# Moving the store of the normalised attention output (x1_scr) from GpSimd's DMA queue to ScalarE's

## The reference

```python
c_kv = h @ W_dkv + b_dkv            # 1024 -> 128
c_q  = h @ W_dq + b_dq
k = c_kv @ W_uk + b_uk              # 16 heads of 48, + 16 rotary from h @ W_kr
v = c_kv @ W_uv + b_uv              # 16 heads of 64
q = c_q @ W_uq + b_uq               # + 16 rotary from c_q @ W_qr
attn = softmax(q k^T / 8) v ; attn = attn @ W_o + b_o
x = layernorm(x + attn)
y = x @ int4_quantised(kernel) + bias + (x @ a) @ b
x = layernorm(x + y)
```

## Time and profile before

| | us |
|---|---|
| median of 2 runs | 3198.26 (3198.25 to 3198.28) |
| the profiled execution | 3201.12 |
| its span on the slowest core (core 3) | 3199.5 |
| spans of the other cores | 3168.2 to 3192.4 |

### The profile page before, as it was taken

The page is one execution under the profiler, slowest core; times in us unless marked ns, Lnnn a source line. Parts: engine busy times, 40 slices in busy tenths (PEclk is TensorE's granted clock), DMA queues, the critical chain, the costliest instruction groups (busy, mean ns, idle before and its releaser), DMA issues.

```text
span 3199.5 us, 40217 instructions; the slowest of 8 cores (3168.2 to 3199.5 us)
## 1 busy us (share of the span) xinstructions
PE 2508.0 (78%) x10584; PEld 787.7 (25%) x10584; DVE 1168.8 (37%) x1494; ACT 2193.9 (69%) x2481; POOL 228.0 (7%) x388
## 2 busy tenths in 40 slices
PE   0545759999788978888888888997889788988733
PEld 0222312222232222222222222222222222222211
DVE  3266311212443244324342443244423343334344
ACT  0233339999678976788679867986788677977700
POOL 3000000000000000000000000000000000010000
PEclk9756669999899998899999989998999899999966
DMA  5432230001212111201220121112111212121221
GB/s 94 112 102 97 80 85 19 22 18 35 75 50 71 35 63 56 75 24 49 73 76 29 45 81 48 58 42 71 57 54 50 69 42 65 36 80 44 65 92 40
DMA packets 90051, 190.27 MB, mean 59 GB/s; under 512 B 18643, under 2 KB 50644, under 8 KB 89588
## 3 DMA queue, kind: packets, MB, share of 16 engines
q1 hardware_dynamic: 47812, 86.48, 9.5%
q0 software_dynamic: 28208, 76.05, 8.0%
q10 hardware_dynamic: 13824, 25.17, 2.1%
HBM read 144.65 MB, written 51.64 MB: 61 GB/s over the span
## 4 chain that ended last, share of the span: by engine, by line
PE 54%; DVE 13%; ACT 11%; issue 10%; DMA 10%; SPq 1%; POOL 0%; DVEq 0%; ACTq 0%; POOLq 0%
PE PS L234 51%; ACT Psb L246 8%; DVE tA L251 3%; DVE bcast_sb L277 3%; PE PS L240 2%; ACT bcast_sb L246 2%; DMA h<-h 2%; DMA bcast_sb<-rden 1%; DVE h L251 1%; DMA rotq_scr<-c0s_sb 1%; DMA x_scr<-tA 1%; DMA rden<-bcast_sb 1%; DVE Qsb L257 1%; DMA wbuf<-W_dq 1%; DVE Psb L257 1%
## 5 line engine op out<-in xcount | busy, mean ns | idle before, releaser
L246 ACT ACTIVATE Psb<-PS 128x1024 bf16<-128x1024 f32 x2048 | 1979.8, 1042 | 476.2 <-PE PS L234 462.5
L234 PE MATMUL PS<-Psb,Vsb 128*65 128x512 bf16 x4096 | 1330.5, 408 | 114.2 <-ACT bcast_sb L246 96.5
L234 PE MATMUL PS<-Qsb,Ksb 64*128 64x512 bf16 x4096 | 831.0, 399 | 93.3 <-ACT Psb L246 85.4
L234 PEld LDWEIGHTS PS<-Qsb,Ksb 64*128 64x128 bf16 x4096 | 221.7, 93 | 960.0 <-issue 957.4
L234 PEld LDWEIGHTS PS<-Psb,Vsb 128*65 128x65 bf16 x4096 | 294.2, 112 | 613.8 <-issue 613.8
L277 DVE RECIPROCAL bcast_sb<-bcast_sb 128x512 f32<-128x512 f32 x64 | 214.4, 3350 | 261.4 <-DMA bcast_sb<-rden 261.4
L251 DVE TENSOR_TENSOR tA<-PS,h 128x512 f32<-128x512 f32 x128 | 88.4, 691 | 566.0 <-PE PS L234 526.8
L240 PE MATMUL PS<-ident_sb,h 128*128 128x128 f32 x512 | 106.6, 367 | 187.1 <-DMA h<-h 120.4
L273 DVE CAST oun_sb<-PS 64x512 bf16<-64x512 f32 x128 | 87.4, 682 | 424.6 <-PE PS L234 422.5
L234 PE MATMUL PS<-wbuf,osb 128*128 128x512 bf16 x512 | 169.0, 417 | 73.6 <-DVE tA L251 57.3
L227 POOL DMA_DIRECT2D rden<-bcast_sb x128 | 63.1, 498 | 1595.0 <-ACT bcast_sb L246 1573.1
(11 more groups left out here) (84 smaller groups left out, 1104.9 us busy)
## 6 DMA issues: line engine op xcount, KB each, us to landing
h<-h SPq DMA_DIRECT2D x64, 512.0 KB, 4.3
wbuf<-wo_p POOLq DMA_DIRECT2D x32, 512.0 KB, 5.9
bcast_sb<-rden POOLq DMA_DIRECT2D x128, 128.0 KB, 2.8
x_scr<-tA POOLq DMA_DIRECT2D x32, 512.0 KB, 3.1
wbuf<-wf_p POOLq DMA_DIRECT2D x32, 512.0 KB, 5.6
h<-x_scr SPq DMA_DIRECT2D x32, 512.0 KB, 3.8
out<-tA ACTq DMA_DIRECT2D x32, 512.0 KB, 2.7
o_dram<-oun_sb ACTq DMA_DIRECT2D x64, 128.0 KB, 1.7
```

Of the source, the lines that this page charges most:

```text
L234: e.matmul(o, l, r, start=s1, stop=s2, tile_position=t, skip_group_check=k)),
L246: e.activation(o, i, f, scale=sc, bias=b)),
```

## The change

The issue of the store of `x1_scr` moves from GpSimd's queue to ScalarE's. Its waits, its semaphore and its data stay. It is executed 32 times, 4 in each block.

```diff
@@ -911,7 +911,7 @@
                 for _ in ln_chain_gen(e2["sDV"], par):
                     yield
                 st["h2_free"][par] = st["sq_free"]
-                xw = dma("gpsimd", x1_scr[128 * sub:128 * (sub + 1), :], tA[:, :],
+                xw = dma("scalar", x1_scr[128 * sub:128 * (sub + 1), :], tA[:, :],
                          sem="qX", waits=[("sDV", st["ln_out"])])
                 st["tA_q"] = ("qX", xw["qX"])
                 x1w_s[sub] = xw["qX"]
```

## The result

The change makes the kernel slower by a little: ratio of the times 1.0046, 95% interval 1.0036 to 1.0056, that is 14.7 us (11.5 to 17.9) on 3198 us. The medians are 3220.8 us over 44 runs and 3204.6 us for the kernel before over 42; both contain runs in which one die had the lower clock, and the ratio leaves those out.

What follows compares the result with a forecast made beforehand. No engine saturated: PE and ACT hand tiles over through two PSUM buffers, so the change acts only through waits. 9.5 + 4.5 - 1.9 = +12.1 us on the profiled 3201.1 gives 3213.2; prediction 3210 us, range 3198 to 3221.

Steps and rivals of the forecast that it cites:

- What is special at sub = 2, and how ACT behaves: Third sub-tile, interleaved blocks: reciprocal delays the LayerNorm multiply; ACT waits, next exponential starts 0.60 us after the multiply's end.
- Cost at sub = 2, +9.5: Seven interleaved blocks: new PE stall of 3.64 us, old wait gone, net +1.72 us each, less 2.5: +9.5 us.
- TensorE's clock, +4.5: After the longer PE stalls at sub = 2: more time at the lower clock, 3 sites, +4.5 us, bounds 0 to 14.
- Sub = 0 and 1: nothing: Interleaved blocks' first two sub-tiles: ACT loses at most 0.45 us a store, covered by projection matmuls; zero.
- Sub = 3: nothing: Interleaved blocks' fourth sub-tile: no reciprocal lies between, ACT's loss of at most 0.45 us is covered; zero.
- The last block, -1.9: Last token block, three times: ACT has nothing else to do, write into tA comes sooner, 3.1 us after multiply; -1.9 us.
- POOL and SP: zero: GpSimd loses 32 issues and waits, but nothing behind them starts earlier with effect; SP's x1_scr loads unaffected; zero.
- only the issue counts: Rival, chance 0.17: ACT's wait at sub = 2 is made good in later slack; 3196 us, or up to 3202.
- The activations pass the wait: Rival, chance 0.05: exponentials behind the store run on, waits for tA shrink or vanish; 3176 to 3190 us.
- The clock decides: Rival, chance 0.2: every new stall brings 6 slow us and other sites' 0.45 is not fully covered; 3214 to 3228 us.

Runs made afterwards that it cites:

- wait_only: Kernel before, all stores on GpSimd's queue, plus a bare wait on ScalarE for the multiply at sub = 2 of the seven interleaved blocks; ratio to before 1.0031.
- recip8_act: The change with the pair's reciprocal and multiply recorded one step later on VectorE, all 32 stores on ScalarE; ratio to the kernel before 0.9930.
- not_sub2: The change with the 7 stores at sub = 2 of the interleaved blocks left on GpSimd, 25 moved; ratio to the kernel before 1.0030.

## Why the prediction was right, step by step

The time lies inside the range (12.1 us were forecast, 14.7 measured, which on 3198.3 makes 3213), and the main mechanism is the forecast one. The median after, 3220.8, would be at the very edge of 3198 to 3221; but the forecast started from two runs at 3198.3, and over 42 runs the kernel before has 3204.6. The parts do not all agree, and the total is good in part by luck, since errors offset each other.

- **What is special at sub = 2, and how ACT behaves**: right. The issue came 0.08 us after the multiply (0.07 said), the exponential 0.57 after (0.60), PE's matmul 1.73 after (1.77), and PE's stalls were 3.52 to 4.88 us over all cores (3.6 to 5.4).
- **Cost at sub = 2, +9.5**: right. Over all cores PE's stalls there rose from 2.5 to 3.8 us a place, and the time of the head pair by 10.8 us in all.
- **TensorE's clock, +4.5**: over-sized. From 16 us before the multiply's end to 16 us behind it, the time at the lower level was 6.8 us a place before and 6.2 after; in the 32 us behind it, 10.0 and 10.2. So the longer stall brings no longer slow stretch that can be seen, and the 10.8 us above contain whatever it brings. The step took the new stretches from two windows, and the windows before had 0 to 3.4 us behind stalls of the same 1.92 us; so wide a spread was no basis for a difference. Its upper bound of 14 is also added up wrongly: the long stalls enter it with 1.3 slow us and the others with half of 6.0; with the half in both it is 9 + 2.6 = 11.6.
- **Sub = 0 and 1: nothing**: right for ScalarE's queue, where the exponentials' delay was covered. **Sub = 3: nothing**: the transposes come 0.6 us later than before, which the step did not foresee. What it costs can't be told: of the 15.0 us of attention, about 1 is left for it and everything else.
- **The last block, -1.9**: right. Three times 17.1 became 16.4 us, -2.1, and the first write into tA comes 2.82 us after the multiply (3.1 said).
- **POOL and SP: zero**: wrong, by 6.2 us at the end and by 3.2 in the third interleaved block. The step counted what waits behind GpSimd's stores, and neither what the engine does when it closes nor its late issues, which fall elsewhere when the sequence gets shorter. The trace of the kernel before shows 6.2 us after the last issue (3193.3 to 3199.5), and no step asked what they are made of.

Sum of what was found: 10.8 + 3.2 + 6.2 - 2.1 = 18.1 us, and with the 1 us that is left over 19, as in the profiles without the first phase; the timed runs say 14.7 (11.5 to 17.9). The forecast had about 10 us too little for GpSimd and what is left over, and 3 too much for sub = 2 with its clock; that, and a timed difference below the profiled one, left a total that looks better than its parts.

Of the rivals, "only the issue counts" failed on wait_only and recip8_act. The rule behind it (the Trainium skill, DMA: Bandwidth & Descriptors, "Issuing engines are not separate DMA queues") holds for the transfer, since the issue-to-landing time changed only from 3.1 to 2.7 us; it doesn't speak of what stands behind the wait on the issuing engine, and at sub = 2 that is the cost. "The activations pass the wait" failed on the first timeline after. "The clock decides" has no support in the times at the lower level above.

## What to carry to other kernels

Before a DMA is moved to another engine's queue, look up when its last wait will be met, and what stands behind it in the new queue at that moment: an idle GpSimd can wait for free, and a ScalarE that feeds TensorE can't. When a wait of 4 us appears between two engines, ask what the third engine did in that time; here a 3.35 us reciprocal that nobody needed yet stood ahead of a 0.75 us multiply that two engines needed, and recording it two steps later was worth 2.3%, five times what the queue of the store was worth.

## What the runs showed of the hardware that was not expected

- GpSimd's closing DRAIN takes 3.25 to 9.79 us, by the sequence of DMAs that its queue has issued, the same on all 8 cores, and it is part of the span: moving 32 DMAs off GpSimd lengthened the end by 6.2 us, and 32 small ones put back removed that. Over the 13 kernels it grows with the number of DMAs since the last late issue (27 and 30: 3.25; 31: 6.11; 35: 6.44; 98: 9.46; 102: 9.79).
- Two or three DMA issues of GpSimd in each run start 2.2 to 3.4 us after what they wait for, always the same numbers in the sequence on all cores (140, 243 and 349 before; 140 and 249 after; 140, 233 and 319 in not_sub2). Where one falls ahead of something that waits, it costs: 3.2 us at one head pair after the change.
- A bare wait on ScalarE lets the next activation start 0.20 us after the awaited instruction's end; with a DMA issue between it is 0.57.
- A store of 512 KB is issued 0.08 us after the awaited multiply from ScalarE and 0.56 us after it from GpSimd.
